# Messages of a graph network: each tile's gather released at a point of its own, and one copy of indices per group

## The chip, the cores and the metric

One Trainium2 chip, one core. The time is device time in microseconds (us) of the whole kernel.

## The reference

A graph of 3125 nodes with 128 features each and 100,000 edges (src, dst), sorted by dst. Two layers follow each other. The first is an attention layer; the second, which the change concerns, computes a message per edge with a network of three matrix products, takes the mean over the edges of each node, and feeds it with the node's features to a small network:

```python
edge_index = jnp.stack([src, dst])
x = _layernorm(x + _L0_gnn_ref(x, edge_index_t, L0_gnn_kernel, L0_gnn_kernel_attention), axis=-1)
# L1_gnn_ref:
row, col = (edge_index[0], edge_index[1])
msg_in = jnp.concatenate([node_features[row], node_features[col]], axis=-1)
h = jax.nn.relu(msg_in @ Wm1 + bm1)
h = jax.nn.relu(h @ Wm2 + bm2)
messages = h @ Wm3 + bm3
agg = jax.ops.segment_sum(messages, col, num_segments=num_nodes)
```

## The kernel before

The first product is taken per node, not per edge: table_a holds each node's share as a source (3125 rows of 256 fp32), table_b its share as a destination. The third product and the mean are moved behind the sum over the edges. What is left per edge is h1 = relu(table_a[src] + table_b[dst]), h2 = relu(h1 Wm2 + bm2) and the sum of h2 over the edges of a node.

`messages` does this for 784 tiles of 128 edges, in 196 groups of GT = 4 tiles. Engines run side by side and meet at semaphores, which count up; a loop body holds GUN = 4 groups (u = 0 to 3), and there are loops of it on every engine.

- **TensorE** works for group m in this order: `hidden2` (two bias matmuls, then h1 times Wm2, each split into a high and a low part: high times high, high times low, low times high; in two halves q = 0, 1, each ending with an increment of h2_summed), `hidden1` of group m+1 (one-hot times a window of table_b, and transposes of the four gathered tiles, L1203; in two halves k = 0, 1 of the features, each ending with an increment of h1_summed), and `aggregate` of group m-1 (24 small matmuls with one-hots of the destinations, L1237, ending with an increment of agg_summed).
- **GpSimd** only gathers: four indirect DMAs per group (L1174), each 128 rows of 1 KB of table_a into ga[:, u, k, :], by the indices idx[:, u, k]. ga has GUN = 4 places, so group g's gathers go to the place of group g-4. GpSimd's waits stand in a queue: what is behind a waiting instruction waits too.
- **ScalarE** copies the indices (`indices`, L1263) and so tells GpSimd that the place is free; it also makes the high part of h1 (`high`, L1270), and the first two bf16 parts of h2 (`part1`, L1274, and `part2`, L1278).
- **VectorE** makes h1's low part (L1357), the rests and the third part of h2 (L1363, L1368), the one-hots (L1347, L1349) and adds the aggregate into agg (`add_sums`, L1388), which waits for agg_summed.
- **SyncE** fetches each group's window of table_b and its destinations (L1154, L1155) after h1_summed.

h1_summed starts at 8, h2_summed at 4 and agg_summed at 2. ScalarE's order in a group is what sets the gathers free before the change:

```python
act.wait_ge(agg_summed, n + u + 1)
part1(n, u, 0)
if not last:
    indices(i + GUN, u, 0)
part1(n, u, 1)
if not (last and u == GUN - 1):
    high(n, u + 1)
if not last:
    indices(i + GUN, u, FETCH)
part2(n, u, 0)
part2(n, u, 1)
```

Of the kernel before, what the change touches and what calls it, by code (L numbers as in the profile page):

```python
# [51 lines left out]
GT = 4  # L52
# [2 lines left out]
GW = 42  # L55
GWM = 3 * GW
GUN = 4
FETCH = 2
NPAD = N + 1 + GW
STEPS = (N + GW) // GW + 1  # L60

# [11 lines left out]
ACT = mybir.ActivationFunctionType  # L73
# [975 lines left out]
def messages(nc, T, wm2, bm2, table_a, table_b, scr_dst, bm3, wm3, bn1, wn1, wn2, bn2, out):  # L1049
# [5 lines left out]
    with ExitStack() as ctx:  # L1055
        def sb(name, shape, dt):
            return ctx.enter_context(nc.sbuf_tensor(name, shape, dt))

        def sem(name):
            return ctx.enter_context(nc.semaphore(name))  # L1060
# [10 lines left out]
        idx = sb("idx", [P, GUN, GT], i32)  # L1071
# [17 lines left out]
        idx_ready = sem("idx_ready")  # L1089
# [6 lines left out]
        h1_summed = sem("h1_summed")  # L1096
        hi_ready = sem("hi_ready")
        lo_ready = sem("lo_ready")
        h2_summed = sem("h2_summed")
# [6 lines left out]
        agg_summed = sem("agg_summed")  # L1106
# [10 lines left out]
        def sweeps(eng, start, body, end):  # L1117


            passes = eng.value_load(T.passes_i[0:1, 0:1], min_val=1, max_val=STEPS)  # L1120
            with eng.Fori(0, passes) as p:
                n0 = eng.snap(p * GROUPS, min_val=0, max_val=STEPS * GROUPS)
                if start:
                    start(n0)
                body(n0, 0, True, False)
                with eng.Fori(GUN, LAST, GUN) as i:
                    i = bounded(i, GUN, LAST - GUN)
                    body(eng.snap(p * GROUPS + i, min_val=0, max_val=STEPS * GROUPS), i, False, False)
                body(eng.snap(p * GROUPS + LAST, min_val=0, max_val=STEPS * GROUPS), LAST, False, True)
                end(p)  # L1130
# [32 lines left out]
        @block.gpsimd  # L1163
        def _(pool):
            pool.iota(third_i[:, :], [[0, 1]], base=0, channel_multiplier=1).then_inc(setup_done, 1)

            def body(n, i, first, last):
                for u in range(GUN):

                    for k in range(GT):  # L1170
                        if k % FETCH == 0:
                            pool.wait_ge(idx_ready, (n + u) * (GT // FETCH) + k // FETCH + 1)
                            pool.sem_inc(pool_order, 1)
                        pool.indirect_dma_start(ga[:, u, k, :], None, table_a,  # L1174
                                                bass.IndirectOffsetOnAxis(ap=idx[:, u, k:k + 1], axis=0)).then_inc(gathered[u][k], 16)

            def end(p):
                pool.wait_ge(tables_next, p + 1)
                pool.sem_inc(pool_order, 1)
            sweeps(pool, None, body, end)  # L1180
# [76 lines left out]
        @block.scalar  # L1257
        def _(act):
            act.sem_inc(h2_summed, 4)
            act.sem_inc(agg_summed, 2)  # L1260

            def indices(i, u, k):
                act.activation(idx[:, u, k:k + FETCH], T.src_idx[:, bass.ds((i + u) * GT + k, FETCH)], ACT.Copy).then_inc(idx_ready, 1)  # L1263

            def high(n, u):

                act.wait_ge(h2_summed, (n + u) * 2 + 2)
                for k in range(2):
                    act.wait_ge(h1_summed, (n + u) * 2 + 2 * GUN + 1 + k)
                    act.activation(h1_hi[:, u % 2, k, :], ps1[u % 2][k][:, :], ACT.Relu).then_inc(hi_ready, 1)  # L1270

            def part1(n, u, q):
                act.wait_ge(h2_summed, (n + u) * 2 + q + 5)
                act.activation(h2[0][:, u % 2, 2 * q:2 * q + 2, :], ps2[q][:, :, :], ACT.Relu).then_inc(part1_ready, 1)  # L1274

            def part2(n, u, q):
                act.wait_ge(rest_ready, (n + u) * 2 + q + 3)
                act.activation(h2[1][:, u % 2, 2 * q:2 * q + 2, :], rest1[:, u % 2, 2 * q:2 * q + 2, :], ACT.Copy).then_inc(part2_ready, 1)  # L1278

            def start(n):  # L1280
                for u in range(GUN):
                    for k in range(0, GT, FETCH):
                        act.activation(idx[:, u, k:k + FETCH], T.src_idx[:, u * GT + k:u * GT + k + FETCH], ACT.Copy).then_inc(idx_ready, 1)
                high(n, 0)

            agg_flat = T.agg[:, :, :].rearrange("p k n -> p (k n)")
            act.activation(agg_flat, T.ident[:, 0:1].broadcast_to([P, 2 * NPAD]), ACT.Copy, scale=0.0).then_inc(agg_cleared, 1)

            def body(n, i, first, last):
                for u in range(GUN):  # L1290

                    act.wait_ge(agg_summed, n + u + 1)
                    part1(n, u, 0)
                    if not last:
                        indices(i + GUN, u, 0)
                    part1(n, u, 1)
                    if not (last and u == GUN - 1):
                        high(n, u + 1)
                    if not last:
                        indices(i + GUN, u, FETCH)  # L1300
                    part2(n, u, 0)
                    part2(n, u, 1)

            def end(p):
                act.wait_ge(tables_next, p + 1)
            sweeps(act, start, body, end)
            update.scalar(act)

# [194 lines left out]
```

## Time and profile before

| | us |
|---|---|
| median of 3 runs (2322.45 to 2332.38) | 2332.14 |
| profiled execution, its own time | 2344.28 |
| its span | 2342.4 |
| TensorE busy | 1865.0 (80%) |
| VectorE busy | 1579.9 (67%) |
| ScalarE busy | 1227.7 (52%) |
| GpSimd busy | 1192.9 (51%) |
| mean granted clock of TensorE | 0.907 |

The busy times are unions of an engine's instructions over the span. The span is made of the index tables and the attention layer, then the loop over the 196 groups of messages, then the update of the nodes. In the names of the rows PE is TensorE's matmuls, DVE VectorE, ACT ScalarE, POOL GpSimd. "issue" as a releaser means that the profile shows nothing that the engine waited for, "remote" that the semaphore moved without an instruction that had just ended.

### The profile page before, as it was taken

What the parts mean: (1) busy time and instruction counts of PE and PEld (TensorE: products, weight loads), DVE (VectorE), ACT (ScalarE), POOL (GpSimd) and SP (SyncE); (2) the same over time, 40 slices, a digit from 0 to 9 for tenths busy, and PEclk for the clock granted to TensorE, in tenths of its full rate; (3) what the DMA queues carried; (4) which work ended last, traced back from release to release, by engine and by line L of the source; (5) the groups of instructions that cost most, each with busy time, mean ns of one, the idle gap of its engine ahead of it and who ended that gap; (6) DMA issues with size and microseconds to landing.
All of it is one profiled execution on the core that took longest, in us unless ns stands there. A gap on an engine that the chain in (4) does not pass through costs nothing.

```text
span 2342.4 us, 53618 instructions
## 1 busy us (share of the span) xinstructions
PE 1865.0 (80%) x15435; PEld 1555.4 (66%) x15435; DVE 1579.9 (67%) x3407; ACT 1227.7 (52%) x2293; POOL 1192.9 (51%) x1204
## 2 busy tenths in 40 slices
PE   4567888777777647888888888888888888888887
PEld 3346666665556436777777777777777777777774
DVE  5678988776666846666666666666666666666676
ACT  3025678877878434454544544444444444545441
POOL 4213466566656235555555555555555555555530
PEclk9899998988788878999998999899998999999999
DMA  2023567776777253333333333333333333333320
GB/s 76 19 52 85 117 131 136 132 135 133 137 136 140 67 154 99 100 100 99 104 101 100 96 103 99 98 99 106 97 99 98 100 98 99 103 100 100 99 58 28
DMA packets 141711, 236.32 MB, mean 101 GB/s; under 512 B 27966, under 2 KB 92562, under 8 KB 141627
## 3 DMA queue, kind: packets, MB, share of 16 engines
q0 software_dynamic: 49632, 142.89, 24.4%
q1 hardware_dynamic: 91994, 92.45, 16.8%
q8 instruction: 35, 0.57, 0.1%
q14 instruction: 50, 0.40, 0.1%
HBM read 185.52 MB, written 10.66 MB: 84 GB/s over the span
## 4 chain that ended last, share of the span: by engine, by line
PE 39%; another core or an unknown queue 10%; issue 6%; ACT 4%; DVE 3%; ACTq 0%; DMA 0%; DVEq 0%; POOL 0%; POOLq 0%
PE ps L1225 10%; PE ps L1219 8%; PE ps L1220 8%; PE ps L1203 5%; PE ps L1211 3%; PE psA L1237 2%; PE ps L1198 2%; DVE rest L1363 2%; ACT h L1274 1%; ACT h_hi L1270 1%; ACT h L1278 1%; PE ps L958 1%; ACT idx L1263 1%; PE ps L969 0%
## 5 line engine op out<-in xcount | busy, mean ns | idle before, releaser
L1174 POOL DMA_INDIRECT ga<-table_a,idx x784 | 791.5, 1010 | 613.3 <-ACT idx L1263 417.6
L1274 ACT ACTIVATE h<-ps 128x512 bf16<-128x512 f32 x392 | 233.1, 596 | 654.2 <-PE ps L1225 416.9
L1219 PE MATMUL ps<-wm_hi,h_hi 128*128 128x256 f32 x1568 | 464.9, 323 | 48.2 <-issue 25.6
L1363 DVE SCALAR_TENSOR_TENSOR rest<-ps,h 128x512 f32<-128x512 f32 x392 | 265.4, 688 | 320.1 <-ACT h L1274 246.2
L587 POOL DMA_INDIRECT head_n<-scr_eye,row_at x250 | 302.2, 1209 | 342.5 <-PE psC L632 259.8
L1220 PE MATMUL ps<-wm_lo,h_hi 128*128 128x256 f32 x1568 | 434.6, 304 | 13.6 <-issue 12.4
L1219 PEld LDWEIGHTS ps<-wm_hi,h_hi 128*128 128x128 f32 x1568 | 331.3, 211 | 91.0 <-ACT h_hi L1270 38.5
L1220 PEld LDWEIGHTS ps<-wm_lo,h_hi 128*128 128x128 f32 x1568 | 332.9, 212 | 28.8 <-issue 27.0
L1225 PE MATMUL ps<-wm_hi,h_lo 128*128 128x256 f32 x1568 | 293.5, 305 | 41.2 <-issue 39.4
L1357 DVE SCALAR_TENSOR_TENSOR h_lo<-ps,h_hi 128x512 fp32r<-128x512 f32 x392 | 260.2, 687 | 49.8 <-ACT h_hi L1270 38.6
L641 PE MATMUL psC<-ring_n,ring_m 128*126 x1180 | 239.0, 332 | 60.1 <-DVE ring_n L830 34.1
L1225 PEld LDWEIGHTS ps<-wm_hi,h_lo 128*128 128x128 f32 x1568 | 244.2, 211 | 46.3 <-issue 44.8
L1270 ACT ACTIVATE h_hi<-ps 128x512 fp32r<-128x512 f32 x392 | 226.4, 599 | 75.3 <-remote 36.3
L1203 PE MATMUL ps<-ident,ga 128*128 128x128 f32 x1568 | 247.0, 278 | 8.5 <-issue 7.8
L1368 DVE TENSOR_TENSOR h<-rest,h 128x512 bf16<-128x512 f32 x392 | 253.4, 687 | 0.1
L641 PEld LDWEIGHTS psC<-ring_n,ring_m 128*126 x1180 | 166.9, 146 | 120.0 <-issue 110.2
L1203 PEld LDWEIGHTS ps<-ident,ga 128*128 128x128 f32 x1568 | 204.4, 145 | 50.5 <-issue 19.3
L1278 ACT ACTIVATE h<-rest 128x512 bf16<-128x512 f32 x392 | 225.2, 629 | 0.2 <-DVE rest L1363 0.2
L728 ACT ACTIVATE stage<-psC 126x626 f32<-126x626 f32 x125 | 85.8, 686 | 231.4 <-PE psC L650 208.4
L830 DVE TENSOR_SCALAR ring_n<-iota_n,edge_keys 128x626 int16 x590 | 206.5, 391 | 0.0
L1237 PE MATMUL psA<-hot_e,h 128*128 128x42 bf16 x4704 | 162.7, 181 | 44.1 <-issue 41.2
L632 PE MATMUL psC<-head_n,head_m 128*126 128x313 bf16 x500 | 119.2, 347 | 94.4 <-DMA head_n<-scr_eye,row_at 82.0
(193 smaller groups left out, 2632.4 us busy)
## 6 DMA issues: line engine op xcount, KB each, us to landing
dstb<-scr_dst SPq DMA_DIRECT2D x196, 126.0 KB
cnt<-stage SPq DMA_DIRECT2D x125, 195.3 KB
cnt<-stage SPq DMA_DIRECT2D x125, 109.9 KB
ga<-table_a,idx POOLq DMA_INDIRECT x784
bw<-table_b SPq DMA_DIRECT2D x196, 63.0 KB
table_b<-cnt SPq DMA_DIRECT2D x12, 336.0 KB
head_n<-scr_eye,row_at POOLq DMA_INDIRECT x250
table_a<-pr SPq DMA_DIRECT2D x12, 224.0 KB
```

The source lines that it names most:

```text
L587: pool.indirect_dma_start(head_n[:, w % 2, s, :], None, scr_eye, bass.IndirectOffsetOnAxis(ap=row_at[:, w % 3, s:s + 1], axis=0)).then_inc ...
L641: last = pe.matmul(bank[0:WME, k, 0:HALF], ring_m[:, bass.ds(slot, 1), :, s].rearrange("p o m -> p (o m)"), ring_n[:, bass.ds(slot, 1), s, ...
L1174: pool.indirect_dma_start(ga[:, u, k, :], None, table_a, bass.IndirectOffsetOnAxis(ap=idx[:, u, k:k + 1], axis=0)).then_inc(gathered[u][k] ...
L1203: last = pe.matmul(bank[:, t * P:(t + 1) * P], ga[:, s, t, k * P:(k + 1) * P], T.ident[:, :], is_transpose=True, start=False, stop=True, s ...
L1219: pe.matmul(ps2[q][:, t % 2, :], hi, w_hi[:, k, :], start=False, stop=True, skip_group_check=True)
L1220: pe.matmul(ps2[q][:, t % 2, :], hi, w_lo[:, k, :], start=False, stop=True, skip_group_check=True)
L1225: last = pe.matmul(ps2[q][:, t % 2, :], h1_lo[:, u % 2, k, t * P:(t + 1) * P], w_hi[:, k, :], start=False, stop=True, skip_group_check=True)
L1270: act.activation(h1_hi[:, u % 2, k, :], ps1[u % 2][k][:, :], ACT.Relu).then_inc(hi_ready, 1)
L1274: act.activation(h2[0][:, u % 2, 2 * q:2 * q + 2, :], ps2[q][:, :, :], ACT.Relu).then_inc(part1_ready, 1)
L1357: dve.scalar_tensor_tensor(h1_lo[:, u % 2, k, :], ps1[u % 2][k][:, :], 0.0, h1_hi[:, u % 2, k, :].bitcast(fp32), ALU.max, ALU.subtract).th ...
L1363: dve.scalar_tensor_tensor(rest1[:, u % 2, 2 * q:2 * q + 2, :], ps2[q][:, :, :], 0.0, h2[0][:, u % 2, 2 * q:2 * q + 2, :], ALU.max, ALU.su ...
L1368: dve.tensor_tensor(h2[2][:, u % 2, 2 * q:2 * q + 2, :], rest1[:, u % 2, 2 * q:2 * q + 2, :], h2[1][:, u % 2, 2 * q:2 * q + 2, :], ALU.sub ...
```

## The change

Each gather but the first of a group gets a wait of its own on GpSimd, and the indices of a group are copied by one instruction in place of two. For group g: tile 0 waits for the copy of its indices, which ScalarE makes after `part1` of the first half of group g-4; tile 1 for the first half of `hidden1` of group g-3; tile 2 for `aggregate` of group g-5, which TensorE does after that `hidden1`; tile 3 for the first half of `hidden2` of group g-3. In the first four groups the tiles 1 to 3 have no wait.

```diff
--- before.py
+++ after.py
@@ -55,7 +55,6 @@
 GW = 42
 GWM = 3 * GW
 GUN = 4
-FETCH = 2
 NPAD = N + 1 + GW
 STEPS = (N + GW) // GW + 1
 
@@ -1164,12 +1163,23 @@
         def _(pool):
             pool.iota(third_i[:, :], [[0, 1]], base=0, channel_multiplier=1).then_inc(setup_done, 1)
 
+            def release(n, u, k):
+
+                if k == 0:
+                    pool.wait_ge(idx_ready, n + u + 1)
+                elif k == 1:
+                    pool.wait_ge(h1_summed, (n + u) * 2 + 3)
+                elif k == 2:
+                    pool.wait_ge(agg_summed, n + u - 2)
+                else:
+                    pool.wait_ge(h2_summed, (n + u) * 2 - 1)
+
             def body(n, i, first, last):
                 for u in range(GUN):
 
                     for k in range(GT):
-                        if k % FETCH == 0:
-                            pool.wait_ge(idx_ready, (n + u) * (GT // FETCH) + k // FETCH + 1)
+                        if k == 0 or not first:
+                            release(n, u, k)
                             pool.sem_inc(pool_order, 1)
                         pool.indirect_dma_start(ga[:, u, k, :], None, table_a,
                                                 bass.IndirectOffsetOnAxis(ap=idx[:, u, k:k + 1], axis=0)).then_inc(gathered[u][k], 16)
@@ -1259,8 +1269,8 @@
             act.sem_inc(h2_summed, 4)
             act.sem_inc(agg_summed, 2)
 
-            def indices(i, u, k):
-                act.activation(idx[:, u, k:k + FETCH], T.src_idx[:, bass.ds((i + u) * GT + k, FETCH)], ACT.Copy).then_inc(idx_ready, 1)
+            def indices(i, u):
+                act.activation(idx[:, u, :], T.src_idx[:, bass.ds((i + u) * GT, GT)], ACT.Copy).then_inc(idx_ready, 1)
 
             def high(n, u):
 
@@ -1279,8 +1289,7 @@
 
             def start(n):
                 for u in range(GUN):
-                    for k in range(0, GT, FETCH):
-                        act.activation(idx[:, u, k:k + FETCH], T.src_idx[:, u * GT + k:u * GT + k + FETCH], ACT.Copy).then_inc(idx_ready, 1)
+                    act.activation(idx[:, u, :], T.src_idx[:, u * GT:(u + 1) * GT], ACT.Copy).then_inc(idx_ready, 1)
                 high(n, 0)
 
             agg_flat = T.agg[:, :, :].rearrange("p k n -> p (k n)")
@@ -1292,12 +1301,10 @@
                     act.wait_ge(agg_summed, n + u + 1)
                     part1(n, u, 0)
                     if not last:
-                        indices(i + GUN, u, 0)
+                        indices(i + GUN, u)
                     part1(n, u, 1)
                     if not (last and u == GUN - 1):
                         high(n, u + 1)
-                    if not last:
-                        indices(i + GUN, u, FETCH)
                     part2(n, u, 0)
                     part2(n, u, 1)
 
```

GpSimd in the loop body, before, from the start of the body; each wait is in brackets behind the instruction that it holds:

```order
L1126 ISA
L1174 DMA ga<-table_a,idx 128x256 [waits idx_ready]
L1174 DMA ga<-table_a,idx 128x256
L1172 REGISTER_ALU
L1174 DMA ga<-table_a,idx 128x256 [waits idx_ready]
L1174 DMA ga<-table_a,idx 128x256
```

The same place after the change:

```order
L1184 DMA ga<-table_a,idx 128x256 [waits idx_ready]
L1171 ISA
L1184 DMA ga<-table_a,idx 128x256 [waits h1_summed]
L1173 REGISTER_ALU
L1184 DMA ga<-table_a,idx 128x256 [waits agg_summed]
L1175 REGISTER_ALU
L1184 DMA ga<-table_a,idx 128x256 [waits h2_summed]
```

The gathers come in the same order; three of four now wait for TensorE itself, and none passes without a wait.

ScalarE in the loop body, before (h_0 is h2's first part, h_1 its second, ps_0 and ps_1 the halves of hidden2):

```order
L1273 ISA [waits agg_summed]
L1274 ACTIVATE h_0<-ps_0 128x512 [waits h2_summed]
L1263 ISA
L1263 ACTIVATE idx<-src_idx 128x2
L1273 REGISTER_ALU
L1274 ACTIVATE h_0<-ps_1 128x512 [waits h2_summed]
L1267 ISA
L1269 REGISTER_ALU [waits h2_summed]
L1270 ACTIVATE h_hi<-ps_10 128x512 [waits h1_summed]
L1269 REGISTER_ALU
L1270 ACTIVATE h_hi<-ps_11 128x512 [waits h1_summed]
L1263 ISA
```

and after:

```order
L1283 ISA [waits agg_summed]
L1284 ACTIVATE h_0<-ps_0 128x512 [waits h2_summed]
L1273 ISA
L1273 ACTIVATE idx<-src_idx 128x4
L1283 REGISTER_ALU
L1284 ACTIVATE h_0<-ps_1 128x512 [waits h2_summed]
L1277 ISA
L1279 REGISTER_ALU [waits h2_summed]
L1280 ACTIVATE h_hi<-ps_10 128x512 [waits h1_summed]
L1279 REGISTER_ALU
L1280 ACTIVATE h_hi<-ps_11 128x512 [waits h1_summed]
L1287 REGISTER_ALU
```

The copy behind part1 has four columns now, and the second one, between h_hi and h_1, is gone.

## Rows read from the trace of the kernel before

**Rows 1.** Windows, the loop: us, busy (count) PE PEld DVE ACT POOL, clock, DMA share, GB/s

```profile
868.39:2269.98 1401.59, 1195.17 (x11678) 1047.45 (x11677) 894.94 (x1750) 682.74 (x1553) 784.06 (x777) 0.92 0.35 99
```

**Rows 2.** Windows, single groups, from bias matmul to bias matmul

```profile
1515.96:1521.05 5.09, 5.09 (x67) 4.73 (x63) 4.56 (x10) 3.60 (x9) 3.17 (x3) 1.00 0.38 113
1521.05:1530.15 9.10, 7.01 (x68) 6.22 (x64) 4.76 (x10) 3.63 (x9) 4.83 (x5) 0.81 0.32 93
1530.15:1535.38 5.23, 5.23 (x68) 4.87 (x63) 4.60 (x10) 3.65 (x9) 3.25 (x4) 1.00 0.42 112
1535.38:1543.10 7.72, 5.77 (x66) 5.11 (x62) 4.69 (x10) 3.56 (x9) 4.08 (x5) 1.00 0.34 93
1506.72:1515.96 9.24, 7.29 (x65) 6.46 (x61) 4.71 (x10) 3.56 (x9) 4.82 (x5) 0.82 0.32 93
```

**Rows 3.** Timeline of TensorE: start, us, engine line op, [idle before, releaser]

```profile
1517.30 0.62 PE L1225 MATMUL ps<-wm_hi,h_lo 128*128 128x256 f32 x4
...
1519.35 0.60 PE L1203 MATMUL ps<-ident,ga 128*128 128x128 f32 x4
...
1520.45 0.76 PE L1237 MATMUL psA<-hot_e,h 128*128 128x42 bf16 x24
...
1524.26 0.28 PE L1225 MATMUL ps<-wm_hi,h_lo 128*128 128x256 f32 x1 [1.11 <-issue]
...
1529.54 0.76 PE L1237 MATMUL psA<-hot_e,h 128*128 128x42 bf16 x24
...
1534.73 0.76 PE L1237 MATMUL psA<-hot_e,h 128*128 128x42 bf16 x24
```

**Rows 4.** Timeline of VectorE, the additions of the aggregate

```profile
1518.59 0.23 DVE L1388 TENSOR_TENSOR agg<-psA,agg 128x84 f32 x1
...
1525.85 0.24 DVE L1388 TENSOR_TENSOR agg<-psA,agg 128x84 f32 x1 [2.08 <-remote]
...
1540.04 0.24 DVE L1388 TENSOR_TENSOR agg<-psA,agg 128x84 f32 x1 [2.01 <-remote]
```

**Rows 5.** Waits of the message loop: us in total, times, longest us

```profile
POOL ga L1174 <- ACT idx L1263: 417.6, 202, 5.2
...
ACT h L1274 <- remote: 221.2, 64, 10.6
...
DVE agg L1388 <- remote: 140.5, 79, 4.7
```

**Rows 6.** Timeline of GpSimd, gathers

```profile
1514.26 0.94 POOL L1174 DMA_INDIRECT ga<-table_a,idx  x1 [0.30 <-issue]
1517.03 1.28 POOL L1174 DMA_INDIRECT ga<-table_a,idx  x1 [1.83 <-ACT idx L1263]
...
1519.87 0.95 POOL L1174 DMA_INDIRECT ga<-table_a,idx  x1 [0.30 <-issue]
1521.12 0.95 POOL L1174 DMA_INDIRECT ga<-table_a,idx  x1 [0.30 <-issue]
1522.37 1.04 POOL L1174 DMA_INDIRECT ga<-table_a,idx  x1 [0.30 <-issue]
1523.72 0.95 POOL L1174 DMA_INDIRECT ga<-table_a,idx  x1 [0.30 <-issue]
...
1528.71 0.94 POOL L1174 DMA_INDIRECT ga<-table_a,idx  x1 [0.30 <-issue]
1531.21 1.28 POOL L1174 DMA_INDIRECT ga<-table_a,idx  x1 [1.56 <-ACT idx L1263]
...
1534.05 0.95 POOL L1174 DMA_INDIRECT ga<-table_a,idx  x1 [0.30 <-issue]
...
1537.98 0.95 POOL L1174 DMA_INDIRECT ga<-table_a,idx  x1 [0.31 <-issue]
```

**Rows 7.** Timeline of ScalarE, copies of indices

```profile
1516.05 0.20 ACT L1263 ACTIVATE idx<-src_idx 128x2 int32 x1
...
1518.45 0.20 ACT L1263 ACTIVATE idx<-src_idx 128x2 int32 x1
```


## The prediction

> **What bounds the kernel now.** I read the profile by stage first. The window of the message loop [rows 1] gives it 1401.6 of the 2342.4 us, 7.15 us for each of its 196 groups, and the change touches nothing outside it. TensorE is busy 1195.2 us of it, at a granted clock of 0.92. Then I read single groups. The windows of neighbouring groups [rows 2] show that there is no such thing as a typical one: 9.24, 5.09, 9.10, 5.23 and 7.72 us, with the same work in each. The 5.09 and 5.23 us groups have TensorE busy without a break at full clock, so 5.2 us is what a group needs. The loop loses 1401.6 - 196 x 5.2 = 382 us in the other groups, and the question is what the change does to that loss.
>
> The timeline of TensorE through the end of a good group and into a bad one [rows 3] shows the loss. The aggregate's 24 matmuls end at 1520.45 + 0.76 = 1521.21. TensorE goes on with the next group for 1.9 us, to 1524.26 - 1.11 = 1523.15, and then stops with nothing to wait for in its program; the profile names it "issue", and shorter stops follow. In two of the three bad groups [rows 2] the granted clock then falls from 2.4 GHz to its lower level, 1.2 GHz, for a part of the group. What that costs is the difference between two of them: 9.24 us at a mean clock of 0.82 and 7.72 us at 1.00, so 1.5 us.
>
> The other engines tell what was stuck. VectorE's addition of the aggregate into agg (L1388) needs only that aggregate. In the good group it runs in its turn at 1518.59; in the bad one it starts at 1525.85 after 2.08 us of idleness, 4.6 us after the last matmul of the aggregate [rows 4]. The profile calls the releaser "remote", because by its records TensorE had long been done. So TensorE's completion counts reach the others late, and after 1.9 us TensorE itself runs into that. In the waits of the whole loop this is no exception: 79 of the 193 additions waited for such a late count, 140.5 us together, and ScalarE's first relu of h2 did so 64 times for 221.2 us [rows 5].
>
> Which groups are hit? GpSimd's gathers [rows 6] against four aggregates. One ended at 1516.12: the last gather before it had been issued from 1514.26 to 1515.20, the next came at 1517.03; on time. One ended at 1521.21: gathers started at 1519.87 and 1521.12, back to back; late by 4.6 us. One ended at 1530.30 (1529.54 + 0.76) [rows 3]: gathers at 1528.71 and then 1531.21; on time. One ended at 1535.49 (from 1534.73): a gather at 1534.05, others behind it at the same pitch; late, VectorE could add at 1540.04 [rows 4]. **A late count goes with a chain of gathers running across the end of the aggregate.** It also ends with that chain: after 1521.21 GpSimd had two more gathers released in advance, at 1522.37 and 1523.72, and the count came 2.13 us after the start of the last; in the other case 1540.04 - 1537.98 = 2.06 us. Gathers cost 1.25 us each back to back (1519.87, 1521.12, 1522.37), 5.0 us of a 5.2 us group, so GpSimd has nearly no slack either. It is not the bound on average (784.1 us busy of 1401.6), but it waits 417.6 us for the indices that ScalarE copies [rows 5], and ScalarE is late because its counts are.
>
> **The change, part by part.**
>
> *One copy of indices instead of two.* One copy a group (196 in all) at 0.20 us [rows 7] leaves ScalarE, 39 us of an engine that is busy 682.7 of 1401.6 us. It sat ahead of part2, for which nobody waits in a good group. Cost: zero, hidden by ScalarE's waits for late counts. Should ScalarE become the bound, it is worth up to 0.2 us a group, 39 us at the most. The remaining copy has 4 columns; no row shows that width, the 2-column one takes 0.20 us and even at twice that it would lie beside GpSimd's gather before.
>
> *Two more waits and two more increments per group on GpSimd.* The gather at 1519.87 [rows 6] has such a wait, for the indices of 1518.45, ahead of it, and the idle time before it is the same 0.30 us as before those without. Satisfied waits cost nothing. A wait that is not satisfied costs the wake-up: indices copied at 1516.05 + 0.20 [rows 7], gather started at 1517.03, so 0.78 us. Bounds 0 and 2 x 0.78 us a group.
>
> *The release points.* Counted from the group's first bias matmul (1515.96) in the good group [rows 3, 7]: first half of h2 done at 1.96; indices copied by 2.69; first half of h1 at 3.99; aggregate at 5.25. With 0.78 us to wake and 1.25 us of pitch, tile 3 of the group before starts at 2.74, tile 0 at 3.99 (behind it), tile 1 at 5.24, tile 2 at 6.49, tile 3 at 7.83, which is 2.74 of the next group. In full speed the four points space the gathers by 1.25, 1.25, 1.25 and 1.34 us. **So the change does not keep a gather away from the aggregate**: tile 0 starts 1.26 us and tile 1 0.01 us before its end, almost the picture of 1521.21 (1.34 and 0.09). I expect a late count in nearly every group.
>
> What it does change is how long the count is late. Tile 2 now waits for that very count, and everything behind it on GpSimd's queue with it. Where two more gathers followed before, none does. By the 2.1 us from the last gather's start, the first late count is 2.1 us late instead of 4.6, and TensorE, which runs on for 1.9 us, loses 0.2.
>
> *Steady state.* From one late count to the next: wake-up 0.78, tiles 2, 3 and 0 at 1.25 each, then 2.1 us from the start of tile 1. That is 0.78 + 3.75 + 2.1 = 6.63 us. TensorE fits into this: 5.2 us of work and a stop of 1.4, its count 3.3 us late, with tile 0 just starting as the aggregate ends, so the picture repeats itself. If the clock falls in that stop, TensorE needs 5.2 + 1.5 = 6.7 us and the stop shrinks by as much; that leaves 6.6 to 6.9. Sum: 196 x (7.15 - 6.63) = 102 us less. From the profiled execution's own 2344.28 us that is 2242; this execution lies 12 us above the median of the runs (2332.14), so 2230.
>
> *Who is kept waiting.* Tile 3 of group g is issued while group g-3 is in h2, and is needed in the h1 of group g, one course and a half later at the least: over 11 us for a path of wake-up, 0.95 us of issue and a landing inside the 2.1 us. No matmul should wait for a gather. SyncE's two transfers keep their wait (h1_summed) and their place.
>
> A rule speaks against all of this. The rows say that the count is late with gathers in flight. The Trainium skill, SBUF — State Buffer, section "Who interferes with whom", says that a DMA never contends with a compute engine and that "PE and ACT never wait on anyone". By that rule the match in time is chance or has a common cause, and the new release points give TensorE nothing: 2332 us. The four aggregates above are on the side of the rows; that every late count is a gather's doing is not shown by them.
>
> **The rivals.**
>
> *A: the gathers miss the aggregate (below 5.9 us a group).* Once TensorE paces GpSimd the course might settle where the aggregate's end falls into a pause, as at 1530.30. At the limit, 5.2 us, the loop is 382 us shorter: 1950 us. Half free and half late groups make (5.2 + 6.63) / 2 = 5.9, 245 us less, 2087. Against: GpSimd needs 5.0 of 5.2 us, so there is no pause to fall into.
>
> *B: no change.* The late counts have another cause, or the change only trades long delays for more numerous short ones, 41% of groups for all of them, at the same mean. 7.15 us a group, about 2332. For it: 6.63 is not far from 7.15, and each 0.25 us of additional wait per group eats half of the gain.
>
> *C: slower, through the aggregate as a release.* If the end of a late count is not set by the last gather, but lasts its 4.6 us anyhow, then now every group meets it, and tile 2's wait on agg_summed holds the queue of GpSimd. The row to price it is the bad group at full clock, 7.72 us: 196 x 0.57 = 112 us more, 2444. It decides from the point where (7.15 - 5.2) / (7.72 - 5.2) = 77% of the groups are hit. For it: both late counts in these rows are 4.6 us, suspiciously equal. Against: the two chains of gathers were equally long too. With the clock down in each group (9.1 us) it would be 2700, which I leave out.
>
> **How the numbers follow.** A measurement of this kernel tells about 0.5% (12 us). The forecast, 5.9 to 7.1 us a group, gets 0.55; A 0.13; B 0.10; C 0.22. Faster is the forecast and A, 0.68; same 0.10; slower 0.22. Low end 2080, half of the groups free, leaving out the better part of A; high end 2400, between the 6.63 + 0.78 us of one more unsatisfied wait (7.41 us, 2383) and C's 2444, leaving out some half of C. GpSimd's other bound, two more wake-ups (8.2 us, 2535), is left out with it: it needs each release to come after the queue has run dry.
>
> **What would show it.** Right: group pitch narrow around 6.6 instead of 5.1 to 9.1; VectorE's addition waiting for a "remote" in most groups, but under 1.5 us each; GpSimd's idle time released by TensorE instead of by idx; granted clock in the loop at 0.95 or more; no gap of 1.1 us on TensorE longer than one per group; L1263's count halved and nothing seen of it. Wrong: additions on time in most groups (A); waits of 2 us and more before the addition in most groups (C); TensorE's transposes (L1203) waiting for a gather, which would mean that the lead was too short.

## The result and the profile after

| | before | changed |
|---|---|---|
| median, us | 2332.26 (2322.45 to 2335.29, 4 runs) | 2238.59 (2229.42 to 2245.74, 4 runs) |
| ratio | | 0.9594, 95% interval 0.9564 to 0.9624 |
| span of the profiled execution | 2342.4 | 2226.5 |

The change made the kernel 4.1% faster; 2230 had been forecast. The windows of the changed kernel, the whole loop and then four neighbouring groups (start and end in us, length, busy time of TensorE's matmuls, weight loads, VectorE, ScalarE and GpSimd with counts, granted clock, DMA share, GB/s):

```profile
860.15:2154.32 1294.17, 1115.53 (x11678) 980.03 (x11677) 909.67 (x1750) 677.34 (x1361) 777.52 (x777) 0.98 0.39 108
```

```profile
1442.52:1449.12 6.60, 5.58 (x67) 4.98 (x63) 4.80 (x10) 3.69 (x8) 3.85 (x4) 1.00 0.37 109
1449.12:1456.02 6.90, 5.61 (x65) 5.03 (x62) 4.75 (x10) 3.48 (x8) 3.92 (x5) 1.00 0.35 104
1456.02:1462.73 6.71, 5.52 (x67) 4.95 (x63) 4.73 (x10) 3.52 (x8) 4.11 (x5) 1.00 0.39 107
1462.73:1468.85 6.12, 5.68 (x67) 4.95 (x63) 4.73 (x10) 3.52 (x8) 3.92 (x4) 1.00 0.41 116
```

The loop lost 1401.6 - 1294.2 = 107 us against [rows 1], most of the difference of the two spans; 8.5 us were lost outside it, which the change does not touch. These are the slowest execution of the kernel before and the fastest of the changed one: the medians differ by 94 us. Where a group took 5.1 or 9.1 us before [rows 2], these four take between 6.1 and 6.9, each at full clock. Measured from bias matmul to bias matmul over the whole loop, the middle half of the 195 pitches (a pitch is the time from one group's start to the next one's) lies between 6.3 and 6.8 us now, and lay between 5.8 and 8.1 before. Seen from TensorE, little of the gain is in its stops: the loop minus its busy time was 1401.6 - 1195.2 = 206 us and is 1294.2 - 1115.5 = 179. The other 80 us are its busy time, with the same matmuls at a clock of 0.98 instead of 0.92 (1195.2 x 0.92 = 1100 and 1115.5 x 0.98 = 1093 us at full clock): the stops have become short and regular, and the clock stays up.

The gathers on GpSimd and VectorE's addition of the aggregate through one such group (start, length, instruction, idle time before it and its releaser):

```profile
1453.39 0.95 POOL L1184 DMA_INDIRECT ga<-table_a,idx  x1 [1.91 <-PE ps L1235]
1454.64 0.95 POOL L1184 DMA_INDIRECT ga<-table_a,idx  x1 [0.30 <-issue]
1455.89 0.95 POOL L1184 DMA_INDIRECT ga<-table_a,idx  x1 [0.30 <-PE ps L1213]
1457.15 1.22 POOL L1184 DMA_INDIRECT ga<-table_a,idx  x1 [0.31 <-issue]
1460.05 0.94 POOL L1184 DMA_INDIRECT ga<-table_a,idx  x1 [1.68 <-PE ps L1235]
```

```profile
1455.42 0.76 PE L1247 MATMUL psA<-hot_e,h 128*128 128x42 bf16 x24
...
1458.37 0.40 PE L1235 MATMUL ps<-wm_hi,h_lo 128*128 128x256 f32 x2 [0.84 <-issue]
```

```profile
1459.30 0.24 DVE L1395 TENSOR_TENSOR agg<-psA,agg 128x84 f32 x1 [0.58 <-remote]
```

The aggregate ends at 1455.42 + 0.76 = 1456.18, with a gather just issued and another to come. Its count reaches VectorE at 1459.30, 3.1 us after that end and 2.15 us after the start of the last gather at 1457.15. (VectorE has other work first: where no count is late, the addition starts 2.45 us after the aggregate's end, as the rows of e5_no_agg_release show below. So "late" in this text counts from the end of the last matmul, and VectorE itself lost 0.58 us here.) Then 0.75 us pass until GpSimd's next one at 1460.05. The period is 1460.05 - 1453.39 = 6.66 us: wake-up, three pitches of 1.25, and 2.15.

The gathers at 1453.39 and 1460.05 are those of tile 2, which wait for the aggregate's count. The profile names L1235, hidden2, as their releaser, because the wait of the gather behind them, for h2_summed, is passed before they start. Which tile a gather belongs to can be told from the semaphore that it increments: in this loop 173 of the 194 gathers of tile 2 came after an idle time of over 0.6 us, and 0, 20 and 8 of the tiles 0, 1 and 3.

The waits of the loop, against [rows 5] (us in total, times, longest):

```profile
POOL ga L1184 <- PE ps L1235: 271.5, 162, 2.0
POOL ga L1184 <- issue: 161.2, 503, 2.1
DVE agg L1395 <- remote: 128.7, 160, 1.5
...
ACT h L1284 <- remote: 70.1, 22, 7.8
...
POOL ga L1184 <- ACT idx L1273: 8.4, 13, 2.3
```

160 of 193 additions now wait for a late count, instead of 79, but none longer than 1.5 us (before: 4.7). ScalarE's waits of that kind fell from 64 to 22. GpSimd waits for TensorE and no longer for the indices (417.6 us before, 8.4 now).

### The profile page after: what moved, and what is told of

The parts are those of the page before. It is cut to its first block, busy times and chain, and to the rows that moved or that the text cites. A ratio compares the mean times of both kernels' runs of the same rounds, so it can differ in the third digit from the quotient of the medians.

```text
span 2226.5 us, 53898 instructions
## 1 busy us (share of the span) xinstructions
PE 1773.2 (80%) x15435; PEld 1484.0 (67%) x15435; DVE 1597.5 (72%) x3407; ACT 1221.3 (55%) x2097; POOL 1177.2 (53%) x1204
## 4 chain that ended last, share of the span: by engine, by line
PE 47%; issue 9%; DVE 3%; another core or an unknown queue 2%; ACT 1%; DVEq 0%; ACTq 0%
PE ps L1235 10%; PE ps L1229 9%; PE ps L1230 8%; PE ps L1213 7%; PE psA L1247 4%; PE ps L1221 4%; PE ps L1208 4%; DVE rest L1370 1%; PE ps L957 1%; DVE h_lo L1364 1%; PE ps L968 0%; PE ps L965 0%; DVE h L1375 0%; PE psA L976 0%
## 5 line engine op out<-in xcount | busy, mean ns | idle before, releaser
L586 POOL DMA_INDIRECT head_n<-scr_eye,row_at x250 | 294.8, 1179 | 345.4 <-PE psC L631 268.8
L1229 PE MATMUL ps<-wm_hi,h_hi 128*128 128x256 f32 x1568 | 432.7, 306 | 49.3 <-issue 41.2
L1230 PE MATMUL ps<-wm_lo,h_hi 128*128 128x256 f32 x1568 | 397.5, 284 | 20.5 <-issue 18.2
L1229 PEld LDWEIGHTS ps<-wm_hi,h_hi 128*128 128x128 f32 x1568 | 299.3, 191 | 100.6 <-issue 72.2
L1235 PE MATMUL ps<-wm_hi,h_lo 128*128 128x256 f32 x1568 | 286.4, 288 | 81.6 <-issue 79.1
L1230 PEld LDWEIGHTS ps<-wm_lo,h_hi 128*128 128x128 f32 x1568 | 300.2, 191 | 37.5 <-issue 36.1
L1235 PEld LDWEIGHTS ps<-wm_hi,h_lo 128*128 128x128 f32 x1568 | 227.4, 191 | 90.0 <-issue 88.1
L1213 PE MATMUL ps<-ident,ga 128*128 128x128 f32 x1568 | 239.7, 274 | 1.1 <-DMA ga<-table_a,idx 0.6
L1208 PE MATMUL ps<-hot_t,bw 126*128 126x512 bf16 x392 | 153.2, 391 | 23.9 <-DVE hot_e L1356 22.9
```

The costliest lines, as they stand in the source:

```text
L586: pool.indirect_dma_start(head_n[:, w % 2, s, :], None, scr_eye, bass.IndirectOffsetOnAxis(ap=row_at[:, w % 3, s:s + 1], axis=0)).then_inc ...
L1208: pe.matmul(bank[:, :], bw[0:GWM, s, k * P:(k + 1) * P], hot_t[0:GWM, s, :], start=True, stop=True, skip_group_check=True)
L1213: last = pe.matmul(bank[:, t * P:(t + 1) * P], ga[:, s, t, k * P:(k + 1) * P], T.ident[:, :], is_transpose=True, start=False, stop=True, s ...
L1229: pe.matmul(ps2[q][:, t % 2, :], hi, w_hi[:, k, :], start=False, stop=True, skip_group_check=True)
L1230: pe.matmul(ps2[q][:, t % 2, :], hi, w_lo[:, k, :], start=False, stop=True, skip_group_check=True)
L1235: last = pe.matmul(ps2[q][:, t % 2, :], h1_lo[:, u % 2, k, t * P:(t + 1) * P], w_hi[:, k, :], start=False, stop=True, skip_group_check=True)
```

## The experiments

Every experiment was run once, unless it says otherwise.

**First four: a chip on which no count is late.** The kernel before, measured beside them on their chip, took 1956.21 us, not 2332. The edits (in e2_no_windows TensorE's and VectorE's waits for the windows are set so that the first four groups' fulfil them):

```diff
 # e1_one_gather (three tiles left out)
-                    for k in range(GT):
+                    for k in range(1):
...
-                                         ga[:, s, t, k * P:(k + 1) * P]
+                                         ga[:, s, 0, k * P:(k + 1) * P]
 # e2_no_windows (SyncE, in the loop)
+                    if not first:
+                        continue
 # e3_short_aggregate (2 matmuls of 24)
-                for t in range(GT):
-                    for c in range(3):
+                for t in range(1):
+                    for c in range(1):
 # e5_no_agg_release
-                    pool.wait_ge(agg_summed, n + u - 2)
+                    pool.wait_ge(h1_summed, (n + u) * 2 + 4)
```

> The changed kernel, but only tile 0 of each group is gathered and TensorE transposes it four times (the other three tiles are left out of the computation). Theory G (a gather running across the end of the aggregate makes TensorE's counts late): the one gather starts 3.5 us after the bias matmul and is over before the aggregate ends at 5.25, so late counts vanish, a group takes 5.2 us instead of 6.64, the kernel 2239 - 196 x 1.44 = 1957 us, granted clock in the loop 1.0. Theory N (the lateness is TensorE's own, or comes from another engine; nothing on a DMA can hold it up): late counts stay in nine of ten groups and the time stays within 2239 +- 20 us.

> The changed kernel without SyncE's two transfers per group in the loop: the windows of table_b and the destinations of the first four groups are used for all (this part of the data is left out). Both transfers start right at the end of the aggregate, so the collision could need them. Theory G (gathers alone): late counts stay, 6.6 us a group, 2239 +- 20 us. Theory S (it takes SyncE's transfers and a gather together): late counts vanish, GpSimd's four gathers at 1.25 us and TensorE's 5.2 us set the group, about 1960 us.

> The changed kernel with 2 of the 24 matmuls of each aggregate (the rest of the sum is left out). Theory G (any count of TensorE is late when a chain of gathers runs across it): the period of 0.78 + 3 x 1.25 + 2.1 = 6.63 us does not contain the aggregate's length, so the time stays within 2239 +- 30 us. Theory M (it takes the burst of 24 short matmuls and their weight loads in 0.6 us together with a gather): no late counts, a group of 5.0 to 5.2 us, 1920 to 1960 us.

> The changed kernel with tile 2 released by the second half of hidden1 instead of by the aggregate, 0.6 us of TensorE's course earlier; the late count then holds back nothing of GpSimd's queue but what waits for h2. Theory H (the gain comes from tile 2 waiting for the late count itself, which keeps two gathers from prolonging it): one more gather follows the aggregate's end, the count is late by 3.3 to 4.6 us, the group 7.0 to 7.9 us, 2310 to 2480 us. Rival P (the gain comes from pacing each gather by TensorE at whatever point): unchanged, 2239 +- 20 us.

Measured, in this order: 1946.26, 1954.68, 1932.13 and 1950.54 us. They decide between none of these theories and their rivals, since there were no late counts to explain. The trace of e5_no_agg_release shows what its absence looks like. The window of the loop, and its waits on GpSimd:

```profile
864.81:1875.28 1010.47, 1010.26 (x11677) 942.33 (x11676) 886.80 (x1750) 685.44 (x1361) 768.07 (x777) 1.00 0.50 138
```

```profile
POOL ga L1184 <- issue: 222.3, 730, 0.3
POOL ga L1184 <- PE ps L1213: 14.0, 46, 0.3
```

TensorE is busy without a break (1010.26 of 1010.47 us), a group takes 5.18 us, and no wait of any engine is ended by a "remote". Yet the gathers run without a pause, across every aggregate. GpSimd:

```profile
1284.71 0.95 POOL L1184 DMA_INDIRECT ga<-table_a,idx  x1 [0.30 <-PE ps L1213]
1285.96 0.95 POOL L1184 DMA_INDIRECT ga<-table_a,idx  x1 [0.30 <-issue]
```

TensorE and VectorE:

```profile
1284.86 0.76 PE L1247 MATMUL psA<-hot_e,h 128*128 128x42 bf16 x24
```

```profile
1288.07 0.23 DVE L1395 TENSOR_TENSOR agg<-psA,agg 128x84 f32 x1
```

This aggregate ended at 1285.62, 0.91 us after the start of one gather and 0.34 us before the next; the addition came in its turn, with no idle time ahead. So on this chip gathers that start before and behind the aggregate's end make no count late.

**The change and two of these again, on another chip.**

> The changed kernel itself, unchanged. In the first four experiments the kernel before took 1956 us on their chip, not 2332, and no count of TensorE was late. Theory C (late counts are a property of the chip or of its surroundings, and the change only shortens them where they occur): on a chip where the kernel before takes 2332 us this one takes 2239; on one where it takes 1956, the two are the same within 0.5%, as GpSimd's 5.0 us and TensorE's 5.2 us of a group are what is left. Theory T (passing: the same chip shows it at one time and not at another): both times mixed within the rounds of one kernel.

> Tile 2 released by the second half of hidden1 instead of the aggregate, once more. Where counts are late: theory H (tile 2's wait for the late count is what shortens it) 2310 to 2480 us; rival P (any pacing by TensorE does it) 2239 +- 20 us. Where they are not: 1950 us, as before.

> One gather of four, once more (the other three tiles are left out). Where counts are late: theory G (gathers across the aggregate's end make them late) about 1957 us; theory N (the gathers have no part in it) 2239 +- 20 us. Where they are not late: 1946 us, as before.

The kernel before took 2369.42 us here (2357.86 to 2377.79, 7 runs in this and the next set, all on this chip) and the changed one 2266.48 (2263.63 to 2267.54, 4 runs): ratio 0.9567, interval 0.9529 to 0.9605, the same gain as in the main measurement. Theory C held in its first half: no run mixed the two levels. Its second half, that the change is worth nothing where the kernel before takes 1956, was not tried with the changed kernel itself; e5_no_agg_release, one wait away from it, was 0.3% faster than the kernel before there (one run of each).

r3_one_gather took 1953.9 us. Its loop and the first of its waits:

```profile
869.94:1879.81 1009.87, 1009.64 (x11677) 941.73 (x11676) 886.70 (x1750) 685.72 (x1361) 182.25 (x192) 1.00 0.22 62
```

```profile
POOL ga L1184 <- ACT idx L1273: 807.5, 191, 7.1
ACT h L1284 <- PE ps L1235: 298.0, 390, 1.8
```

With three of four gathers gone, no "remote" is left, the clock is 1.00, and the group takes 5.18 us, on the same chip where it took 6.78 with them (1322.79 us of loop over 195 pitches). That is theory G's outcome and rules out N: **the late counts go away with the gathers, on this chip.** It does not tell their number from their bytes (62 GB/s against 105), nor GpSimd's work of issuing them from the transfers.

It does narrow theory G. The gather that is left starts 1.82 us before the end of the aggregate (1284.03 + 0.76 = 1284.79), and its rows have landed 2.7 us after its start by the page, at about 1285.7. So a transfer is under way when the aggregate ends, and still VectorE's addition comes in its turn, 2.45 us after that end:

```profile
1282.97 0.95 POOL L1184 DMA_INDIRECT ga<-table_a,idx  x1 [4.24 <-ACT idx L1273]
```

```profile
1284.03 0.76 PE L1247 MATMUL psA<-hot_e,h 128*128 128x42 bf16 x24
```

```profile
1287.24 0.24 DVE L1395 TENSOR_TENSOR agg<-psA,agg 128x84 f32 x1
```

```profile
ga<-table_a,idx POOLq DMA_INDIRECT x196, 2.7
```

What is missing, against the changed kernel, is a gather that starts around or behind the aggregate's end, with others ahead of it. The runs do not separate these two.

r2_no_agg_release took 2296.47 us (the changed kernel's four runs lie within 4 us of each other): between the outcomes of H and P, so neither held whole. Of the 103 us of the change, 73 stay when tile 2 does not wait for the late count. Why shows in a group of it, gathers and additions:

```profile
1479.84 0.94 POOL L1184 DMA_INDIRECT ga<-table_a,idx  x1 [2.10 <-ACT idx L1273]
1481.08 0.95 POOL L1184 DMA_INDIRECT ga<-table_a,idx  x1 [0.30 <-PE ps L1213]
1482.33 0.95 POOL L1184 DMA_INDIRECT ga<-table_a,idx  x1 [0.30 <-issue]
1483.58 1.40 POOL L1184 DMA_INDIRECT ga<-table_a,idx  x1 [0.30 <-issue]
1486.69 0.94 POOL L1184 DMA_INDIRECT ga<-table_a,idx  x1 [1.71 <-PE ps L1235]
```

```profile
1485.80 0.25 DVE L1395 TENSOR_TENSOR agg<-psA,agg 128x84 f32 x1 [1.06 <-remote]
```

The chain is again four long and then stops, now with tile 2's gather as the last (by the semaphores, 185 of tile 3's gathers came after an idle time of over 0.6 us, and 2 of tile 2's): tile 3 waits for a count of hidden2, which is late with the aggregate's. The period is 1486.69 - 1479.84 = 6.85 us, 0.89 to wake, 3.74, and 2.22 from the last start to the addition. Either of the two counts that come late here, the aggregate's or hidden2's, ends the chain when it stands in GpSimd's queue, the aggregate's 0.2 us a group earlier. Those of hidden1 mostly do not: 13 of tile 1's gathers waited.

**Four more on the same chip, where counts are late.**

> The changed kernel without SyncE's two transfers per group in the loop (the first four groups' windows are used for all). On a chip where the kernel before takes 2330 to 2370 us. Theory G (gathers alone make counts late): 6.6 us a group, within 20 us of the changed kernel there (2239 to 2266). Theory S (SyncE's transfers, which start right at the aggregate's end, are needed too): no late counts, about 1960 us. On a chip where the kernel before takes 1956 it says nothing (1955, as before).

> The changed kernel with 2 of the 24 matmuls of each aggregate (the rest of the sum is left out). Where counts are late: theory G (any count is late when a chain of gathers runs across it): the period of 0.78 + 3 x 1.25 + 2.1 us does not contain the aggregate, 2210 to 2270 us. Theory M (the burst of 24 short matmuls and their weight loads is needed): 1930 to 1960 us. Where they are not: 1932, as before.

> The kernel before with one copy of indices per group behind part1 and all four gathers behind that one wait: the copy's part of the change alone, without the release points. The forecast gave the copy itself nothing. Where counts are late: all four gathers are released at once and none waits for TensorE, so the chain after a late count is up to four gathers long: not faster than the kernel before, 1.00 to 1.08 of its time. A rival (the saved copy is what helped) says 0.96 of it. Where counts are not late: the same within 0.5%.

> The changed kernel with the aggregate's 24 matmuls dealt out among the ten matmuls of hidden1, three before each transpose; the same result. Where counts are late: theory M (the burst is needed) says that they vanish, about 1960 us; theory G says that they stay, since the last of them still ends with a chain of gathers in flight, and the period is GpSimd's 6.6 us: 2220 to 2270 us. Where they are not late: 1950 us, TensorE has the same work.

e4 and e6 are these edits, the first of the kernel before:

```diff
 # e4_one_copy_alone
-FETCH = 2
+FETCH = 4
...
-                    if not last:
-                        indices(i + GUN, u, FETCH)
 # e6_spread_aggregate (in hidden1; some(count) issues so many of the 24)
                     for t in range(GT):
+                        if between:
+                            between(3)
```

| | us | against the changed kernel's 2266 |
|---|---|---|
| r4_no_windows | 2250.99 | -15 |
| r5_short_aggregate | 2263.85 | -3 |
| e6_spread_aggregate | 2307.34 | +41 |
| e4_one_copy_alone | 2442.53 | +176; +73 against the kernel before (1.031) |

r4_no_windows: SyncE's transfers are not needed for a late count; theory S fell. Its loop, with a quarter of the bytes gone, is hardly shorter:

```profile
869.95:2176.11 1306.16, 1114.30 (x11678) 980.43 (x11676) 916.09 (x1750) 684.21 (x1361) 771.05 (x777) 0.98 0.27 78
```

r5_short_aggregate: the time is theory G's, and M fell, but the picture is not the one that I had in mind. Its additions no longer wait; the late counts have moved to hidden2:

```profile
ACT h L1284 <- remote: 174.0, 53, 5.2
PEld ps L1221 <- DVE rest L1370: 160.1, 104, 4.9
```

```profile
867.54:2190.02 1322.48, 1063.78 (x7409) 919.81 (x7408) 879.85 (x1749) 657.74 (x1360) 789.81 (x777) 0.91 0.38 105
```

They are fewer and longer, and the clock is down to 0.91. The pitch of 6.6 us that theory G reckoned with is not there: 86 of the 195 pitches are under 5.5 us and 47 over 8. That the time came out in G's range is therefore no support for its formula. So without the burst of 24 short matmuls counts are still late, but other ones. e6_spread_aggregate shows late counts without the burst, too: ScalarE waits 123 times for a late count of hidden2, 317.5 us, against 7 times, 25.2 us, in the changed kernel on this chip (r1_change_again). It is 41 us slower than with the burst, slower than the 2270 that G allowed. That is not all to be put to late counts: none of its pitches is under 6.0 us, where the changed kernel reaches 5.1, and its TensorE is busy 1189 us instead of 1107. What the same edit costs where no count is late was not measured.

```profile
ACT h L1291 <- remote: 317.5, 123, 8.5
```

```profile
ACT h L1284 <- remote: 25.2, 7, 7.2
```

e4_one_copy_alone: the copy's part of the change, alone, costs 73 us. All four gathers are now free at the earlier of the two points. ScalarE's making of h1's high part waits 76 times for a late count, 123.6 us, where it was 32 times and 36.3 us before (on the chip of the main measurement), and the clock in the loop is 0.89. **All of the gain is the release points'**: on top of the one copy they are worth 176 us.

```profile
ACT h_hi L1270 <- remote: 123.6, 76, 3.0
```

```profile
870.04:2369.11 1499.07, 1216.94 (x11678) 1055.86 (x11676) 896.40 (x1750) 666.10 (x1361) 763.31 (x777) 0.89 0.33 93
```

**The last one, of the chain's length.** The edit is `for k in range(3)` on GpSimd, with tile 2 transposed twice.

> The changed kernel with three gathers per group (tile 3 is not gathered, tile 2 is transposed twice). On a chip where counts are late. Formula theory (a group is wake-up 0.78, then the chain of gathers released behind the late count at 1.25 us each, then 2.1 us from the last one's start): one link less, 0.78 + 2 x 1.25 + 2.1 = 5.38 us, a hair above TensorE's own 5.2, so 2266 - 196 x 1.25 = 2021 us where the changed kernel takes 2266. Rival E (with 1.25 us of slack in GpSimd the aggregate's end falls into a pause and the late counts go altogether): 1954 us, as with one gather. Rival F (the lateness has a length of its own, 3 us or more, as soon as a gather is in flight): 6.2 us a group or more, 2180 us or more.

It came to a chip where the kernel before takes 1955.07 us and took 1950.01. Nothing is decided by it: whether a chain of three gives 5.38 us a group, or no late counts, stays open.

## Why the prediction was right

- *Where the loss was.* Right. 5.2 us was taken as what a group needs; 5.18 us was measured wherever counts were on time. The forecast put a kernel without late counts at 1950 us, and the kernel before takes 1955 to 1956 on a chip where none is late.
- *The copy of indices, priced at nothing.* The 4-column copies took 197 ns each, no more than the 2-column ones. ScalarE's busy time in the loop fell by 5.4 us (682.7 to 677.3) and not by the 39 of the forecast, since the copies overlap its other instructions in the record. But a release is more than its time: alone, it costs 73 us (e4_one_copy_alone). The forecast treated copy and release points as separate terms and had no term for the first without the second.
- *The release points do not keep a gather from the aggregate.* Right: 160 of 193 additions late, "nearly every group".
- *The steady state, 0.78 + 3.75 + 2.1 = 6.63 us, count 3.3 us late.* Measured 6.66 in the group above (0.75 + 3.76 + 2.15, 3.1 us late), and 1294.17 / 195 = 6.64 over the loop. The terms were right one by one in the changed kernel. That of 2.1 us was luckier than it looked: it came from two groups of the kernel before, and over all 79 late additions of that kernel the time from the last gather's start has a median of 1.8 us and lies between 2.0 and 2.3 in 33 of them. In the changed kernel it lies there in 138 of 160. What the forecast called a landing inside these 2.1 us was wrong: a gather's rows had landed 2.7 us after its start in r3_one_gather. With a lead of over 11 us this cost nothing. The forecast divided the loop by 196 groups where there are 195 pitches, 0.04 us of each 7.15.
- *The sum.* 102 us had been forecast and 94 were measured between the medians. That 2230 lies 9 us from the measured 2238.59 is as good as the terms allow. TensorE did not run on for the 1.9 us of the forecast in the group above but for 1.35 (1458.37 - 0.84 - 1456.18), and the sum did not depend on it.
- *The clock.* The forecast left open whether it would fall in the stop. It hardly did (0.98), and from TensorE's side this is 80 of the 107 us. The period is GpSimd's, so a lower clock would have been absorbed, as the forecast reckoned; the runs don't show that case for the changed kernel.
- *Tile 2's wait for the late count as the cause.* Half right. Without it 73 of 103 us remain (r2_no_agg_release), because tile 3's wait for hidden2 also ends the chain, one gather later. The step that said "where two more gathers followed before, none does" holds for one more gather too.
- *The lead.* Right: TensorE's transposes waited 0.5 us in total in the changed loop.

Of the rivals, A needed the aggregate to fall into a pause, and 6% of the pitches are under 5.5 us. C (a lateness with a length of its own, 7.72 us a group) did not come: in the changed kernel the count was 3.1 us late in the group shown and the pitch 6.64. B had two halves. That short delays in every group would cost as much as long ones in some fell with the 4.1%. The other, that the late counts are not the gathers' doing, leaned on a rule: the Trainium skill, SBUF — State Buffer, section "Who interferes with whom", says that a DMA never contends with a compute engine and that TensorE never waits on anyone. On the chip of r1_change_again the measurement decides against this reading of it: 2266 us with four gathers a group, 1954 with one, the other engines' work unchanged. That section speaks of ports of SBUF; whether it is there that a count is held up, the runs do not show. On the chip of the first four experiments TensorE waited for nobody, at a higher rate of transfers (138 GB/s).

What stays open: why counts are late on some chips and not on others; what on the way from TensorE's last write to the semaphore is held up; whether it is the number of gathers, their bytes, or GpSimd's issuing of them; and whether 5.18 us a group can be had where counts are late. No version in this study came near it there with all four gathers.

## What to carry to other kernels

A completion that the profile puts down to "remote", with the producer long done, is a loss that no busy time shows; look at what was in flight when it should have come. Where a stall feeds on work that was released in advance, releasing each piece by the progress of the stalled engine itself can cap the stall, here from 4.6 us to 3.1 in the groups shown, and keep the clock up. Fewer and earlier releases did the opposite (e4_one_copy_alone). Before tuning against such a stall, run the kernel on another chip: this loss of 380 us of 2332 was not there on two other chips, and a change that gains 4% on one may gain nothing on the next.

## What the hardware showed that was not expected

- The kernel before took 1956 and 1955 us on two chips, 2369 on a third and 2332 in the main measurement; no set of runs mixed the levels.
- In the main measurement a count of TensorE came 4.6 us behind its last matmul [rows 3, 4]; TensorE went on for another 1.9 us before it stopped, 1.35 us in the group of the changed kernel.
- On the chip of r3_one_gather, a gather whose rows landed behind the aggregate's end did not make its count late (2.45 us from that end to the addition, as where no count is late).
- A gather of 128 rows of 1 KB occupied GpSimd for 0.95 us, at a pitch of 1.25; the same on the chip without late counts. One that had to wait for a late count started 0.75 us (the changed kernel) and 0.89 us (r2_no_agg_release) after the addition that waited for the aggregate's.
- Removing 22 of 24 short matmuls from each aggregate of the changed kernel gained 3 us where counts were late (2264 against 2266). Where they were on time it took 1932 us; the changed kernel itself was not run there, e5_no_agg_release took 1951.
